# First value tile's depthwise 3x3 convolution: nine VectorE taps and one centring matmul in place of nine diagonal-weight matmuls

## The chip, the cores and the metric

One core of one Trainium2 chip runs the whole program. The metric is the device time of one execution in microseconds (us). The kernel before ran three times: 114.6, 115.24 and 115.32 us, a median of 115.24 us.

## What is computed

The input x has 16 x 16 tokens of 192 channels (12 heads of 16). Two attention blocks run one after the other, each on the group-normalised x and each with x added at the end. Only the first block has the convolution that this document is about. Cut to what matters, for one image:

```python
qkv = gn(x) @ w_qkv.T + b_qkv                      # 256 tokens x 576
q, k, v = split into 12 heads of 16 channels, each a 16 x 16 picture
q = layer_norm(dwconv3x3(q, w_pool_q)) * g_q + b_q # norm over the 16 channels of a head
k = layer_norm(dwconv3x3(k, w_pool_k)) * g_k + b_k
v = layer_norm(dwconv3x3(v, w_pool_v)) * g_v + b_v
attn = softmax(q k^T / 4 + rel_h(q) + rel_w(q))    # 256 x 256 per head
x = x + (attn v + q) @ w_proj.T + b_proj
# the second block has no convolution: LoRA-corrected qkv, the same attention
```

The depthwise convolution multiplies each channel's zero-padded 18 x 18 picture by nine weights at nine shifts and adds the nine products. The layer norm first takes the mean over the 16 channels of a head away ("centring"), which is a multiplication by a fixed 128 x 128 matrix, `centre`.

## The kernel before, in words

Everything lies with channels on partitions and the 256 tokens in the free dimension. The 576 channels of q, k and v are five tiles: A (q, heads 0 to 7), B (k, heads 0 to 7), D (64 rows of q and 64 of k, the last four heads of each), C (v, heads 0 to 7, "the first value tile") and E (v, the last 64 rows). Each engine has its own program, an order written out by hand, and the engines meet at semaphores. Each tile of the first block goes through these steps:

- TensorE projects it (`project`, L739); ScalarE adds the bias and writes it into the padded picture `pad` (`pad_tile`, L446).
- The convolution and the centring. For A and C TensorE does both at once (`convolve`, L750): nine accumulating matmuls whose weights are `centre` with its rows scaled by one tap weight each. VectorE builds these matrices (`tap_matrices`, L612), nine for A and nine for C. For B VectorE does the nine taps itself (`taps`: L635 for the first, L638 for the other eight, each of which adds to the result of the one before and waits for it), and TensorE centres the result with one matmul (`centre_tile`, L781). For D VectorE does five taps and GpSimd four (`convolve_pool`, L311, L316, L319), for E GpSimd does all nine.
- ScalarE squares the centred tile (`tile_stats`, L351), TensorE averages over the head (`variance`, L763), ScalarE takes ln and exp (`tile_rstd`, L356, L358), and VectorE multiplies (`normalise`, L547 and L549) into `full`.
- For q and k, ScalarE and VectorE split `full` in two parts, `hi` (`high`, L452) and `lo` (`low`, L651).

A float32 matmul shows as two records of the trace, so nine matmuls are 18 records.

The attention of a block has three stages of four heads and a last stage. Stage (0, 0) is the first stage of the first block. TensorE's order in it is: `pick_unit` for q (L821, L822; waits for `lo` of A), then what stands under position 0, `rel_unit` 0 and 1 (L840, L843; the relative position terms), `pick_unit` for k, what stands under position 4, four `score` calls (L856). `rel_unit` 0 waits until both ScalarE (L363) and VectorE (`move`, L555) have moved the picked q. ScalarE and VectorE write the position terms beside q (`rel_high`, L368, and `rel_low`, L562). `score` waits for them and for the moved k. VectorE then takes row maxima (`maximum`, L567). `warm_up` (L724) issues matmuls whose results nobody uses.

VectorE's order around the change is: the nine matrices for A; the nine taps of B, each with one matrix of C after it; `normalise(A)`; two casts (L658, L659); `low(A)`, which waits for ScalarE's `high(A)`; taps 0 and 1 of D; then stage (0, 0): `move` q, `normalise(B)`, `low(B)`, `rel_low` twice, `move` k, taps 2 and 3 of D, two maxima, tap 4 of D, two maxima; then `normalise(C)` and stage (0, 1), which begins with `move` q again.

TensorE's convolution of C stands in three pieces: two matmuls before stage (0, 0), three at its position 0 (between `pick_unit` and `rel_unit`), and four at position 4 (between `pick_unit` for k and the scores). After stage (0, 0) come `variance(C)` and `centre_tile(D)`, which waits for the fifth tap of D, then stage (0, 1).

Of the kernel before, what the change touches and what calls it, by code (L numbers as in the profile page):

```python
# [75 lines left out]
def attention_blocks(nc, x_t, w_qkv0, w_qkv1, consts, hots, vectors, neg_hot, rel, lora, v_bias1, w_proj, w_proj_q, out_t):  # L76
    with ExitStack() as ctx:
        def sb(name, shape, dt=F32):
            return ctx.enter_context(nc.sbuf_tensor(name, shape, dt))

        def sem(name):
            return ctx.enter_context(nc.semaphore(name))
# [33 lines left out]
        taps_m = sb("taps_m", [128, 2, TAPS, 128])  # L116
# [4 lines left out]
        conv = sb("conv", [128, 2, TOK])  # L121
# [61 lines left out]
        vtaps_set = sem("vtaps_set")  # L183
# [9 lines left out]
        conv_step = [sem("conv_step_k"), sem("conv_step_d")]  # L193
# [316 lines left out]
        def _(dve):  # L510
# [97 lines left out]
            def tap_matrices(v, first, last):  # L608

                for k in range(first, last):  # L610
                    w = vec[:, TAP0 + 9 * (A, C)[v] + k:TAP0 + 9 * (A, C)[v] + k + 1]
                    dve.tensor_scalar(taps_m[:, v, k, :], centre, w, None,  # L612
                                      ALU.mult).then_inc(vtaps_set if v else qtaps_set, 1)

            tap_matrices(0, 0, TAPS)
# [10 lines left out]
            def taps(t, first, last):  # L626

                s = (B, D).index(t)
# [24 lines left out]
            for k in range(TAPS):  # L653
                taps(B, k, k + 1)
                tap_matrices(1, k, k + 1)
# [4 lines left out]
            low(A)  # L660
            taps(D, 0, 2)
# [57 lines left out]
        def _(pe):  # L719
# [23 lines left out]
            def convolve(t, v, first, last):  # L743

                r = ROWS[t]
                if first == 0:
                    pe.wait_ge(qtaps_set if v == 0 else vtaps_set, TAPS)
                    pe.wait_ge(padded, order0.index(t) + 1)
                for k in range(first, last):
                    mm = pe.matmul(cen_ps[t][0:r, :], taps_m[:, v, k, 0:r],  # L750
                                   pad[:, t, k // 3:k // 3 + SIDE, k % 3:k % 3 + SIDE],
                                   start=(k == 0), stop=(k == TAPS - 1))
                    if k == TAPS - 1:
                        mm.then_inc(centred, 1)
# [10 lines left out]
            def centre_tile(t):  # L765

                r = ROWS[t]
                if t == B:
                    pe.wait_ge(conv_step[0], TAPS)
                    pe.wait_ge(lora_c, 1)  # L770
                    parts = [conv[:, 0, :]]
                elif t == D:
# [258 lines left out]
            convolve(A, 0, 0, TAPS)  # L1031
# [6 lines left out]
            convolve(C, 1, 0, 2)  # L1038
# [10 lines left out]
            stage(0, 0, {0: lambda: convolve(C, 1, 2, 5), 4: lambda: convolve(C, 1, 5, TAPS)})  # L1049
# [110 lines left out]
```

## Time and profile before

| what | value |
|---|---|
| three runs | 114.6, 115.24, 115.32 us |
| median | 115.24 us |
| span of the profiled execution, first to last instruction | 111.6 us |
| median less span | 3.6 us |
| instructions | 2106 |
| TensorE matmul busy in the span | 99.6 us |
| VectorE busy | 64.0 us |
| ScalarE busy | 51.2 us |
| GpSimd busy | 31.0 us |

The profile is one execution. Beside its span no own total is listed for it; the 3.6 us lie between its span and the median of the three runs. A matmul's end in the trace is modelled, so the busy time of TensorE says little of how close it is to its limit; the chain of waits says more. The granted clock is shown as a share of 2.4 GHz: 1.00 is 2.4 GHz and 0.50 is 1.2 GHz.

### The profile page before, as it was taken

Reading aid. Unit: us, or ns where it says so; the run is one execution under the profiler, and the core shown is the slowest. Engines: PE = TensorE matmul, PEld = TensorE weight load, DVE = VectorE, ACT = ScalarE, POOL = GpSimd, SP = SyncE. Lnnn points to the kernel's source line nnn. Section 1 sums busy time; section 2 is a strip of 40 time slices with the busy share of each in tenths; the row PEclk is TensorE's granted clock in tenths of the full one; section 3 lists DMA queues with packets and bytes.
Section 4 is the critical chain, followed back from the end, with each engine's and each line's share of the span. In section 5 each row is a group of like instructions: output and inputs, shape, how many; then the busy total and the mean of one; then the engine's idle time right before and its main releaser. Section 6 shows DMA issues by size and latency. Waiting matters only on the chain.

```text
span 111.6 us, 2106 instructions
## 1 busy us (share of the span) xinstructions
PE 99.6 (89%) x830; PEld 72.2 (65%) x833; DVE 64.0 (57%) x132; ACT 51.2 (46%) x115; POOL 31.0 (28%) x45
## 2 busy tenths in 40 slices
PE   5762999999996999999999999799989999989790
PEld 2211888478885888668657655498659778846550
DVE  0479879767969694944380034455796295580130
ACT  4010181764414793555634642155255648824621
POOL 8269140299999999000000000000000000000000
PEclk9995579999679999999999999999999999999999
DMA  3999930000000000000000000000000000000002
GB/s 74 317 293 301 221 28 0 0 3 6 0 0 0 0 9 0 0 0 6 0 0 0 0 0 6 0 0 0 0 0 6 0 0 6 0 0 0 0 6 71
DMA packets 2826, 3.77 MB, mean 34 GB/s; under 512 B 305, under 2 KB 2225, under 8 KB 2817
## 3 DMA queue, kind: packets, MB, share of 16 engines
q0 software_dynamic: 784, 0.79, 6.3%
q1 hardware_dynamic: 1280, 1.41, 4.6%
q10 hardware_dynamic: 752, 1.44, 4.5%
q8 instruction: 7, 0.11, 0.5%
q14 instruction: 3, 0.02, 0.0%
HBM read 3.44 MB, written 0.20 MB: 33 GB/s over the span
## 4 chain that ended last, share of the span: by engine, by line
PE 78%; DVE 10%; ACT 5%; DMA 3%; issue 2%
PE bank L907 10%; PE bank L750 9%; PE bank L739 9%; PE bank L843 6%; PE bank L840 6%; PE bank L882 5%; PE bank L856 4%; PE bank L895 4%; PE bank L883 4%; DVE xn L541 4%; PE bank L821 4%; DVE mx L567 3%; DMA x<-x_t 3%; PE bank L724 3%; PE bank L822 3%; PE bank L781 2%
## 5 line engine op out<-in xcount | busy, mean ns | idle before, releaser
L567 DVE TENSOR_REDUCE mx<-bank 128x2 fp32r<-128x512 f32 x24 | 15.0, 683 | 5.7 <-PE bank L856 5.7
L378 ACT ACTIVATE pt<-bank 128x512 f32<-128x512 f32 x24 | 13.0, 594 | 7.5 <-PE bank L883 7.3
L882 PE MATMUL bank<-qs,ks 128*128 128x256 f32 x48 | 13.4, 310 | 0.3 <-ACT pt L378 0.2
L739 PE MATMUL bank<-xn,w 96*128 96x256 f32 (+1 forms) x40 | 10.1, 443 | 3.6 <-DVE xn L541 3.6
L562 DVE SCALAR_TENSOR_TENSOR qs<-qs,vec,bank 64x512 fp32r<-64x512 f32 x12 | 8.8, 738 | 6.7 <-ACT qs L368 6.7
L883 PE MATMUL bank<-mt,nhot_r 128*128 128x256 f32 x48 | 11.9, 281 | 0.0
L316 POOL TENSOR_SCALAR tap_p<-pad,vec 64x256 f32<-64x256 f32 (+1 forms) x11 | 10.8, 977 | 0.0
L750 PE MATMUL bank<-pad,taps_m 128*128 128x256 f32 x36 | 10.7, 453 | 0.0
L882 PEld LDWEIGHTS bank<-qs,ks 128*128 128x128 f32 x48 | 9.0, 187 | 2.5 <-ACT pt L378 1.8
L724 PE MATMUL bank<-warm 128*128 128x512 bf16 x28 | 9.0, 443 | 1.5 <-POOL warm L275 1.3
L739 PEld LDWEIGHTS bank<-xn,w 96*128 96x128 f32 (+1 forms) x40 | 6.0, 190 | 6.6 <-issue 4.0
L368 ACT ACTIVATE qs<-bank 64x512 fp32r<-64x512 f32 x12 | 7.1, 591 | 6.0 <-PE bank L843 6.0
L750 PEld LDWEIGHTS bank<-pad,taps_m 128*128 128x128 f32 x36 | 8.3, 233 | 1.5
L883 PEld LDWEIGHTS bank<-mt,nhot_r 128*128 128x128 f32 x48 | 9.0, 188 | 0.1
L574 DVE TENSOR_TENSOR on<-os_,srec 128x256 f32<-128x256 f32 x4 | 1.7, 417 | 12.0 <-ACT srec L389 12.0
L843 PE MATMUL bank<-qs,rel_w 64*32 64x32 f32 x192 | 8.3, 194 | 0.0
L319 POOL TENSOR_TENSOR conv_p<-conv_p,tap_p 64x256 f32<-64x256 f32 (+1 forms) x11 | 8.0, 724 | 0.9
L840 PE MATMUL bank<-qs,rel_w 64*64 64x64 f32 x96 | 7.6, 222 | 0.6 <-issue 0.5
L856 PE MATMUL bank<-ks,qs 128*128 128x256 f32 x48 | 7.7, 299 | 0.0
L840 PEld LDWEIGHTS bank<-qs,rel_w 64*64 64x64 f32 x96 | 6.5, 135 | 1.6 <-ACT ks L363 0.7
L821 PE MATMUL bank<-hi,pick 128*128 128x256 f32 x24 | 7.5, 338 | 0.0
L843 PEld LDWEIGHTS bank<-qs,rel_w 64*32 64x32 f32 x192 | 7.3, 111 | 0.0
(103 smaller groups left out, 170.7 us busy)
## 6 DMA issues: line engine op xcount, KB each, us to landing
ks<-hots POOLq DMA_DIRECT2D x1, 768.0 KB, 9.2
wp<-w_proj ACTq DMA_DIRECT2D x1, 576.0 KB, 8.1
w<-w_qkv SPq DMA_DIRECT2D x1, 432.0 KB, 8.6
w<-w_qkv SPq DMA_DIRECT2D x1, 288.0 KB, 4.8
cst<-consts ACTq DMA_DIRECT2D x1, 256.0 KB, 5.0
nhot<-neg_hot ACTq DMA_DIRECT2D x1, 256.0 KB, 5.8
x<-x_t SPq DMA_DIRECT2D x1, 192.0 KB, 3.2
wpq<-w_proj_q ACTq DMA_DIRECT2D x1, 192.0 KB, 8.9
```

What stands on the lines that cost most here:

```text
L378: act.activation(pt[:, h, :, :], key_banks[h % 2][:, :].rearrange("p (k n) -> p k n", k=QT), ACT.Exp).then_inc(exped[b], 1)
L567: dve.tensor_reduce(mx[:, h, :], ring_bank(h // 4, 4 + h % 4)[:, :].rearrange("p (q n) -> p q n", q=QT), AXX, ALU.max).then_inc(maxed[b], 1)
L724: pe.matmul(to[:, :], warm[:, 0:128], warm[:, :], start=True, stop=True)
L739: mm = pe.matmul((qkv_ps if b == 0 else qkv1_ps)[i][p:p + width, :], w[:, k, col:col + width], xn[:, k, :], start=(k == 0), stop=(k == 1))
L750: mm = pe.matmul(cen_ps[t][0:r, :], taps_m[:, v, k, 0:r], pad[:, t, k // 3:k // 3 + SIDE, k % 3:k % 3 + SIDE], start=(k == 0), stop=(k == ...
L821: pe.matmul(dst, pick[:, v, i:i + 2, :], hi[:, place3[t], :], start=True, stop=False)
L840: pe.matmul(out[:, 64 * i:64 * i + 64], rel_w[64:128, 2 * b, SIDE - 1 - y, 0:64], heads[:, :, y, :], start=True, stop=False, skip_group_ch ...
L843: mm = pe.matmul(by_x[:, x], rel_w[64:128, 2 * b + 1, SIDE - 1 - x, 0:32], heads[:, x, 8 * r:8 * r + 8, :], start=False, stop=True, skip_g ...
L856: mm = pe.matmul(ring_bank(g, n)[:, q * TOK:(q + 1) * TOK], qs[:, h, q * 128:(q + 1) * 128], ks[:, h, :], start=True, stop=True)
L882: pe.matmul(dst, ks[:, h, k * 128:(k + 1) * 128], qs[:, h, :], start=True, stop=False)
L883: mm = pe.matmul(dst, nhot_r[:, j, :], mt[:, g, :], start=False, stop=True)
L907: mm = pe.matmul(y_ps[t], weights, moving, start=first_y[b][t], stop=stop, skip_group_check=True)
```

## The change

VectorE builds no matrices for C. It does nine taps for C itself, six after the taps of B and ahead of `normalise(A)`, three after `low(A)` and ahead of the taps 0 and 1 of D. The result goes to a third slot of `conv`. TensorE's nine matmuls for C go: the two ahead of stage (0, 0) leave nothing, the three at position 0 leave one `warm_up` matmul, the four at position 4 leave one centring matmul that waits for the nine taps. The taps of B follow each other with nothing between them. A's convolution stays with TensorE.

```diff
--- before.py
+++ after.py
@@ -113,12 +113,12 @@
         b_row = lo_w[:, 2 * DIM + 32:].rearrange("p (b n) -> p b n", b=2)
         wp = sb("wp", [128, 2, HG, DIM])
         wpq = sb("wpq", [128, 2, DIM])
-        taps_m = sb("taps_m", [128, 2, TAPS, 128])
+        taps_m = sb("taps_m", [128, TAPS, 128])
         pick = sb("pick", [128, 4, 8, 64], F32R)
         warm = sb("warm", [128, 512], mybir.dt.bfloat16)
 
         pad = sb("pad", [128, 5, PADDED, PADDED])
-        conv = sb("conv", [128, 2, TOK])
+        conv = sb("conv", [128, 3, TOK])
         conv_p = sb("conv_p", [128, 2, TOK])
         tap_p = sb("tap_p", [128, 2, TOK])
         cen_e = sb("cen_e", [64, TOK])
@@ -180,7 +180,6 @@
         ones_set = sem("ones_set")
         picks_set = sem("picks_set")
         qtaps_set = sem("qtaps_set")
-        vtaps_set = sem("vtaps_set")
         rel_hi = sem("rel_hi")
         rel_split = sem("rel_split")
         rel_set = sem("rel_set")
@@ -190,7 +189,7 @@
         lora_w = sem("lora_w")
         w1_set = sem("w1_set")
         padded = sem("padded")
-        conv_step = [sem("conv_step_k"), sem("conv_step_d")]
+        conv_step = [sem("conv_step_k"), sem("conv_step_d"), sem("conv_step_v")]
         p_tap = sem("p_tap")
         p_sum = sem("p_sum")
         e_copied = sem("e_copied")
@@ -605,14 +604,9 @@
             dve.wait_ge(d_cst, 16)
             dve.wait_ge(d_vec, 16)
 
-            def tap_matrices(v, first, last):
-
-                for k in range(first, last):
-                    w = vec[:, TAP0 + 9 * (A, C)[v] + k:TAP0 + 9 * (A, C)[v] + k + 1]
-                    dve.tensor_scalar(taps_m[:, v, k, :], centre, w, None,
-                                      ALU.mult).then_inc(vtaps_set if v else qtaps_set, 1)
-
-            tap_matrices(0, 0, TAPS)
+            for k in range(TAPS):
+                w = vec[:, TAP0 + 9 * A + k:TAP0 + 9 * A + k + 1]
+                dve.tensor_scalar(taps_m[:, k, :], centre, w, None, ALU.mult).then_inc(qtaps_set, 1)
 
             dve.wait_ge(d_rel, 16)
             dve.tensor_copy(relt_hi[64:128], relt[64:128]).then_inc(rel_hi, 1)
@@ -625,7 +619,7 @@
 
             def taps(t, first, last):
 
-                s = (B, D).index(t)
+                s = (B, D, C).index(t)
                 dst = conv[:, s, :].rearrange("p (a c) -> p a c", a=SIDE)
                 for k in range(first, last):
                     src = pad[:, t, k // 3:k // 3 + SIDE, k % 3:k % 3 + SIDE]
@@ -650,14 +644,14 @@
                 dve.wait_ge(hi_set[0], i + 1)
                 dve.tensor_tensor(lo[:, i, :], full[:, t, :], hi[:, i, :].bitcast(F32), ALU.subtract).then_inc(lo_set[0], 1)
 
-            for k in range(TAPS):
-                taps(B, k, k + 1)
-                tap_matrices(1, k, k + 1)
+            taps(B, 0, TAPS)
+            taps(C, 0, 6)
             normalise(A)
             dve.wait_ge(d_nhot, 16)
             dve.tensor_copy(ident_r[:], ident).then_inc(id_set, 1)
             dve.tensor_copy(nhot_r[:], nhot[:].rearrange("p (j n) -> p j n", j=4)).then_inc(id_set, 1)
             low(A)
+            taps(C, 6, TAPS)
             taps(D, 0, 2)
 
             def k_in():
@@ -740,18 +734,14 @@
                                        start=(k == 0), stop=(k == 1))
                 mm.then_inc(projected[b], 1)
 
-            def convolve(t, v, first, last):
-
-                r = ROWS[t]
-                if first == 0:
-                    pe.wait_ge(qtaps_set if v == 0 else vtaps_set, TAPS)
-                    pe.wait_ge(padded, order0.index(t) + 1)
-                for k in range(first, last):
-                    mm = pe.matmul(cen_ps[t][0:r, :], taps_m[:, v, k, 0:r],
-                                   pad[:, t, k // 3:k // 3 + SIDE, k % 3:k % 3 + SIDE],
+            def convolve(t):
+
+                pe.wait_ge(qtaps_set, TAPS)
+                pe.wait_ge(padded, order0.index(t) + 1)
+                for k in range(TAPS):
+                    mm = pe.matmul(cen_ps[t], taps_m[:, k, :], pad[:, t, k // 3:k // 3 + SIDE, k % 3:k % 3 + SIDE],
                                    start=(k == 0), stop=(k == TAPS - 1))
-                    if k == TAPS - 1:
-                        mm.then_inc(centred, 1)
+                mm.then_inc(centred, 1)
 
             def variance(t):
                 r = ROWS[t]
@@ -769,6 +759,9 @@
                     pe.wait_ge(conv_step[0], TAPS)
                     pe.wait_ge(lora_c, 1)
                     parts = [conv[:, 0, :]]
+                elif t == C:
+                    pe.wait_ge(conv_step[2], TAPS)
+                    parts = [conv[:, 2, :]]
                 elif t == D:
                     pe.wait_ge(conv_step[1], D_SPLIT)
                     pe.wait_ge(p_sum, TAPS - D_SPLIT)
@@ -1028,14 +1021,13 @@
             pe.wait_ge(d_w0, 32)
             project(0, 0, A, w0)
             project(0, 1, B, w0)
-            convolve(A, 0, 0, TAPS)
+            convolve(A)
             project(0, 2, C, w0)
             variance(A)
             project(0, 3, D, w0)
             centre_tile(B)
             project(0, 4, E, w0)
             variance(B)
-            convolve(C, 1, 0, 2)
 
             def q_and_e():
                 pe.wait_ge(w1_set, 2)
@@ -1046,7 +1038,7 @@
                 variance(E)
                 add_input(0, 0)
 
-            stage(0, 0, {0: lambda: convolve(C, 1, 2, 5), 4: lambda: convolve(C, 1, 5, TAPS)})
+            stage(0, 0, {0: lambda: warm_up(1, bank[7]), 4: lambda: centre_tile(C)})
             variance(C)
             centre_tile(D)
             warm_up(1, bank[5])
```

## Rows read from the trace of the kernel before

**Rows 1.** The page: TensorE clock granted, 40 slices of 2.79 us, in tenths

```profile
PEclk9995579999679999999999999999999999999999
```

**Rows 2.** The page: the chain that ended last, by engine and line

```profile
PE 78%; DVE 10%; ACT 5%; DMA 3%; issue 2%
PE bank L907 10%; PE bank L750 9%; PE bank L739 9%; PE bank L843 6%; PE bank L840 6%; PE bank L882 5%; PE bank L856 4%; PE bank L895 4%; PE bank L883 4%; DVE xn L541 4%; PE bank L821 4%; DVE mx L567 3%; DMA x<-x_t 3%; PE bank L724 3%; PE bank L822 3%; PE bank L781 2%
```

**Rows 3.** That chain in order of time, 18 to 40 us: start us, us, what

```profile
23.23 0.86 PE bank L750 x4
...
24.68 1.30 PE bank L750 x6
...
26.06 0.62 PE bank L840 x8
...
29.02 3.40 PE bank L750 x8
...
32.70 1.29 DVE mx L567 x2
33.98 0.61 DVE conv L638
...
37.76 0.58 PE bank L840 x8
```

**Rows 4.** VectorE in order of time: start us, us, what, [idle before]

```profile
14.75 0.48 DVE L635 TENSOR_SCALAR conv<-pad,vec 128x256 f32<-128x256 f32 x1 [1.19 <-ACT pad L446]
...
19.29 0.28 DVE L612 TENSOR_SCALAR taps_m<-cst,vec 128x128 f32<-128x128 f32 x1
19.48 0.48 DVE L638 SCALAR_TENSOR_TENSOR conv<-pad,vec,conv 128x256 f32<-128x256 f32 x1
...
20.94 0.42 DVE L547 TENSOR_TENSOR nrm<-bank,rstd 128x256 f32<-128x256 f32 x1 [0.78 <-ACT rstd L358]
21.40 0.41 DVE L549 TENSOR_SCALAR full<-nrm,vec 128x256 f32<-128x256 f32 x1
...
23.45 0.42 DVE L651 TENSOR_TENSOR lo<-full,hi 128x256 fp32r<-128x256 f32 x1 [0.96 <-ACT hi L452]
23.79 0.82 DVE L635 TENSOR_SCALAR conv<-pad,vec 128x256 f32<-128x256 f32 x1
24.65 0.58 DVE L638 SCALAR_TENSOR_TENSOR conv<-pad,vec,conv 128x256 f32<-128x256 f32 x1
25.27 0.69 DVE L555 CAST qs<-bank 64x512 fp32r<-64x512 f32 x1
...
30.39 1.24 DVE L638 SCALAR_TENSOR_TENSOR conv<-pad,vec,conv 128x256 f32<-128x256 f32 x2
32.70 1.29 DVE L567 TENSOR_REDUCE mx<-bank 128x2 fp32r<-128x512 f32 x2 [1.07 <-PE bank L856]
```

**Rows 5.** ScalarE in order of time, the same columns

```profile
19.55 0.48 ACT L446 ACTIVATE pad<-bank,vec 128x256 f32<-128x256 f32 x1 [0.48 <-PE bank L739]
...
28.27 0.59 ACT L368 ACTIVATE qs<-bank 64x512 fp32r<-64x512 f32 x1 [0.42 <-PE bank L843]
```

**Rows 6.** GpSimd in order of time, the same columns

```profile
21.69 1.04 POOL L311 TENSOR_SCALAR conv_p<-pad,vec 128x256 f32<-128x256 f32 x1 [6.62 <-ACT pad L446]
22.72 0.92 POOL L316 TENSOR_SCALAR tap_p<-pad,vec 128x256 f32<-128x256 f32 x1
```

**Rows 7.** TensorE in order of time, the same columns

```profile
10.44 3.75 PE L739 MATMUL bank<-xn,w 96*128 96x256 f32 x8 [2.99 <-DVE xn L541]
...
20.90 0.70 PE L781 MATMUL bank<-conv,cst 128*128 128x256 f32 x2
```

**Rows 8.** Stretches: busy of each engine, granted clock, DMA share, GB/s

```profile
8.50:9.00 0.50, 0.00 (x0) 0.00 (x0) 0.50 (x1) 0.00 (x0) 0.50 (x1) 0.50 0.93 289
26.00:28.30 2.30, 2.21 (x49) 2.13 (x49) 1.78 (x4) 0.97 (x3) 2.05 (x4) 1.00 0.04 7
29.00:32.30 3.30, 3.30 (x10) 2.58 (x9) 2.53 (x4) 0.59 (x1) 3.13 (x5) 0.50 0.00 0
```

## The prediction, made before the changed kernel ran

> **What bounds the kernel now.** I read four views in this order. First the page's chain by engine and line: TensorE is 78% of it, and L750, the convolution matmuls for A and C, is 9% of the span [rows 2]. That makes the change look like a gain, so the next question is what stands beside those matmuls. The chain in order of time shows C's three pieces: 0.86 us at 23.23 (4 records), 1.30 us at 24.68 (6 records) and 3.40 us at 29.02 (8 records) [rows 3]. Third, VectorE in order of time over the same stretch: from 14.75 to the first row maximum at 32.70 it is nearly full. Three idle times matter there: 0.78 us ahead of `normalise(A)`, 0.96 ahead of `low(A)`, and 1.07 ahead of the maxima, the only one that C's matmuls cause [rows 4]. And `rel_unit` 0 at 26.06 starts just after VectorE has moved q (25.27 + 0.69 = 25.96) [rows 3, 4]: the 1.30 us piece only fills a wait for VectorE. Last, the granted clock: it is low in slices 10 and 11 [rows 1], and in 29.00 to 32.30 it is 0.50 against 1.00 during the position terms before it [rows 8]. So the 3.40 us piece runs at 1.2 GHz, 0.425 us a record against 0.217 in the 1.30 us piece. After the maxima the chain goes through tap 4 of D (VectorE) back to TensorE [rows 3].
>
> So in 20 to 37 us VectorE and TensorE bound the kernel in turn, and the change takes work from TensorE and gives it to VectorE there.
>
> **The change, part by part.** All times are those of the profiled execution.
>
> *Taps of B without the matrices.* Between two taps stands a matrix today; the pitch is 0.59 us (19.29 and 19.48 are the last such pair, the tap before them starts 0.59 before 19.48) [rows 4]. Without it each tap waits for the one before. No row has two free dependent taps in succession, but `normalise` shows a dependent pair: 20.94 + 0.42 = 21.36, and the next starts at 21.40, a gap of 0.04 [rows 4]. I take 0.48 + 0.04 = 0.52. Bounds: 0.59 (the matrix costs nothing) and 0.40 (the issue interval of a tap ahead of a matrix). B then ends at 14.75 + 8 x 0.52 + 0.48 = 19.39 instead of 19.96. Nobody gains: `centre_tile(B)` starts at 20.90 in TensorE's own order [rows 7].
>
> *Six taps of C ahead of `normalise(A)`.* They need C's picture, which ScalarE writes from 19.55 for 0.48 [rows 5]: start about 20.07. Of the 0.57 us won on B nothing is left. GpSimd starts its own taps at 21.69 [rows 6], and VectorE's taps are slower from then: two in 1.24, 0.62 each [rows 4]. Three at 0.52 and three at 0.62 end at about 23.47. `normalise(A)` starts there instead of at 20.94: 2.5 late. Bounds for the nine C taps: 0.40 each (no gap, no slowdown) and 0.82 each, the longest tap of the trace (23.79) [rows 4].
>
> *`normalise(A)` to `low(A)`.* The two multiplications take 0.87 us to 24.34, the two casts 0.7 more to about 25.05 (now from 21.81 to 23.45 - 0.96 = 22.49 [rows 4]). ScalarE's `hi` of A (about 0.48, as the ScalarE row of that tile size [rows 5]) is then done under the casts, so the 0.96 wait goes. `low(A)` starts at 25.05 instead of 23.45: 1.6 late. TensorE's `pick_unit` waits for that.
>
> *Three taps of C, then taps 0 and 1 of D, ahead of `move` q.* 3 x 0.62 = 1.86 from 25.45 gives 27.3; the D taps take 1.44 as now (23.79 to 25.23), to 28.75. `move` q starts at 28.77 instead of 25.27 and `rel_unit` 0 at 29.55 instead of 26.06: **3.5 late**. This is the step that counts. TensorE can't hide it: behind the waiting `rel_unit` are the pick of k and the scores, all of which need it or come after it in its order. ScalarE's `rel_high` and GpSimd (whose results for D and E nobody awaits here) don't set it.
>
> *Nine matmuls out of TensorE.* The first piece (0.86) lay ahead of a pick that now waits for `low(A)`: worth nothing. The second (1.30) lay in the wait for `move` q: nothing, and its warm-up of one matmul is hidden. The third, 3.40, gives way to one centring matmul (two records, 0.70 at the most [rows 7], twice that at the low clock). Without it the scores could have started once k had been moved, just ahead of 30.39, and VectorE's next two D taps ran until 31.63 (30.39 + 1.24) [rows 4]. So what the third piece costs today is the idle 1.07 us up to 32.70, and that is what is won. The other 2.3 us of it lay beside VectorE's work.
>
> *Sum with the clock high.* 3.5 - 1.07 = +2.4 us at the maxima. Nothing later absorbs it: two maxima, tap 4 of D, two maxima, `normalise(C)` and `move` q run back to back on VectorE and `rel_unit` at 37.76 awaits them [rows 3]; after it the chain is TensorE nearly throughout [rows 2].
>
> *The clock.* In the changed kernel TensorE idles from the end of `variance(B)` (23.23, where C's first piece stands now) to 29.55, but for one pick (0.6, now 24.09 to 24.68) and a warm-up [rows 3]. The trace has one idle time of that kind: 2.99 us ahead of 10.44 [rows 7], and within it, at 8.50, the clock is at 0.50 [rows 8]; it is still low in slice 4 [rows 1]. It fell also after 2.3 us of position terms [rows 8]. So I take it that the two `rel_unit` run at 1.2 GHz. No row has them there. They take 2.2 us now (26.06 to ScalarE's start behind them at 28.27 [rows 3, 5]). Bounds: nothing more, and 2.1 more (0.425 against 0.217 a record, times 1.96, as for C's own matmuls [rows 3]). I take **+1.9**, near the upper end, because the only matmuls seen at both clocks scale so, and a little less because some of the 2.2 us is latency. It is on the path: ScalarE's second `rel_high` at 28.27 was released by them (L843 [rows 5]), and `rel_low` and `move` k follow. The scores at half clock lie beside VectorE's D taps and maxima.
>
> *Sum:* 3.5 - 1.07 + 1.9 = +4.3. The profiled span 111.6 becomes 115.9. The median of the runs lies 3.6 above the span, so 115.24 + 4.3 = **119.5 us**.
>
> *A rule weighed.* The GpSimd rows and the taps beside them show taps of 0.62 instead of 0.48 [rows 4, 6], some 0.1 us for each. The Trainium skill ("SBUF — State Buffer", section "SBUF: two separate sides") says of the port pair that VectorE and GpSimd share that one of them holds it for its whole instruction, and that it holds also for a VectorE instruction with two SBUF inputs against a GpSimd one that reads SBUF. That speaks against the change; what it would make here is the third rival.
>
> **The rivals.**
>
> 1. *The clock stays high.* For it: the clock is not shown falling at once in an idle time, and the picks and the warm-up matmul stand in this one. Against: 8.50. Time: 115.24 + 2.4 = 117.6.
>
> 2. *TensorE is the bound after all, and the change is faster.* The place is the start of `rel_unit` 0. It decides if VectorE moves q less than 1.07 us late; then the loss is smaller than the idle time that goes. For it: 78% TensorE in the chain [rows 2]. At the extreme all 5.56 us of L750 for C go and 0.9 of centring and warm-up come: 110.6. Against: with C's taps at 0.40 each, `normalise(A)` starts at 22.5, `low(A)` at 24.1, and with 0.4 each for the five taps after it `move` q at 26.5, 1.2 late. Even the low bound is 115.24 + 0.15 = 115.4 with the clock high. To be faster, taps would have to be cheaper than any row shows.
>
> 3. *Each contended tap waits out a GpSimd instruction.* Six taps of C run beside GpSimd instructions of some 0.9 us [rows 6]; met half-way through they would wait 0.45 instead of the 0.1 counted, 6 x 0.35 = 2.1 more: 121.6. For it: the tap of 0.82 at 23.79. (This is the rule of the Trainium skill's page "SBUF — State Buffer" named above; the trace agrees with it in that tap only.) Against: 0.58 and twice 0.62 in the same traffic [rows 4].
>
> 4. *The low clock lasts.* If the picks, the scores and the next pair of position terms also run at 1.2 GHz, and the latter (2.1 us now, from 37.76) take the same +1.9, the time is 121.4. Against: the clock rose both times after some us of dense matmuls (slices 5 and 12 [rows 1]), and centring, scores and variance are such.
>
> **How the numbers follow.** 0.50 for the forecast (119.5; its own range 118.4 to 120.5), 0.25 for the first rival (117.6), 0.05 for the second with its low bound, 0.08 for the third, 0.12 for the fourth. The range 116.8 to 121.5 takes in the high clock with slightly cheaper taps and reaches the two dear cases. A measurement of this kernel can tell about 1%, 1.15 us, from no change. Slower by more than that: 0.92; within 1%: 0.05, the low bound of the second rival; faster: 0.03.
>
> **What would show it.** In the changed profile: the first C tap at about 20.1 released by ScalarE's `pad`; free taps 0.52 apart and contended ones 0.62; `normalise(A)` at 23.5; no wait ahead of `low(A)`; `move` q near 28.8 and `rel_unit` 0 near 29.6; two idle times of TensorE, of 2 and 3 us, both ended by VectorE (L651, L555); a clock of 0.50 at 29.6 and `rel_unit` pairs of about 4 us; the maxima at about 37 instead of 32.7 with no idle time ahead of them; everything after 37.76 later by one constant. It is wrong if `rel_unit` 0 starts before 27.5, if the shift at the maxima is under 1 us, or if a wait after 40 us swallows it.

## The result, and the profile after

The changed kernel has a median of 121.62 us in four runs (120.32 to 122.14) against 115.28 us of the kernel before in the same rounds: ratio 1.058, interval 1.047 to 1.069. The forecast was 119.5 us with a range of 116.8 to 121.5. The direction was right and the time lies just above the range. A second set of rounds (below, `after_again`) gave 1.067, interval 1.058 to 1.075. The change costs some 6%, where I had forecast 3.7%. A ratio here compares the runs of each kernel that lie within 1.5% of its own fastest, in the same rounds.

The page of the changed kernel first. What was L739 is L733, L750 is L742, L781 is L774, L840 and L843 are L833 and L836, L856 is L849, L895 is L888, L907 is L900, L635 is L629, L638 is L632.

```profile
span 118.9 us, 2074 instructions
...
PE   5795999931989999999999999899989999999790
...
PEclk9999999985555899999999999999997559999999
...
PE 72%; DVE 13%; ACT 6%; issue 4%; DMA 3%
PE bank L900 10%; PE bank L733 6%; PE bank L849 6%; PE bank L833 6%; PE bank L836 6%; PE bank L875 5%; PE bank L888 4%; PE bank L876 4%; PE bank L742 4%; DVE xn L540 3%; PE bank L814 3%; DMA x<-x_t 3%; PE bank L718 3%; PE bank L815 2%; DVE conv L632 2%
```

In the chain L742, now A's convolution alone, has 4% where L750 had 9% [rows 2]: the work did leave the chain. "issue" went from 2% to 4% and VectorE from 10% to 13%. In the TensorE row slices 8 and 9 (counted from 0) show 3 and 1 tenths: the waits. And the clock row has two low spells, slices 8 to 13 and 30 to 32, where the kernel before had slices 3 to 5 and 10 to 11 [rows 1].

The first spell is what the prediction had priced. The chain in order of time (start, us, what):

```profile
20.40 0.36 DVE conv L629
...
27.50 1.97 issue
29.47 1.03 PE bank L833 x8
30.50 0.83 PE bank L836 x16
31.33 0.88 PE bank L833 x8
32.21 0.84 PE bank L836 x16
...
41.96 0.58 PE bank L833 x8
```

VectorE's taps are in the chain now (20.40). `rel_unit` 0 starts at 29.47 behind 1.97 us of "issue" that stand for the wait for VectorE's move of q; the two `rel_unit` take 1.03 + 0.83 + 0.88 + 0.84 = 3.58 us instead of 2.2 [rows 3]. Stage (0, 1) starts at 41.96 instead of 37.76 [rows 3]: 4.2 us late, where 4.3 was forecast.

VectorE in the same stretch (start, us, what, idle before):

```profile
15.44 4.13 DVE L632 SCALAR_TENSOR_TENSOR conv<-pad,vec,conv 128x256 f32<-128x256 f32 x8
20.40 0.35 DVE L629 TENSOR_SCALAR conv<-pad,vec 128x256 f32<-128x256 f32 x1 [0.83 <-ACT pad L445]
...
23.37 0.42 DVE L546 TENSOR_TENSOR nrm<-bank,rstd 128x256 f32<-128x256 f32 x1
...
24.44 0.94 DVE L652 CAST nhot_r<-nhot 128x512 fp32r<-128x512 f32 x1
25.31 0.41 DVE L645 TENSOR_TENSOR lo<-full,hi 128x256 fp32r<-128x256 f32 x1
25.64 2.00 DVE L632 SCALAR_TENSOR_TENSOR conv<-pad,vec,conv 128x256 f32<-128x256 f32 x3
...
28.67 0.69 DVE L554 CAST qs<-bank 64x512 fp32r<-64x512 f32 x1
...
36.39 1.29 DVE L566 TENSOR_REDUCE mx<-bank 128x2 fp32r<-128x512 f32 x2
```

Eight dependent taps of B take 4.13 us, 0.516 each (forecast 0.52). `normalise(A)` starts at 23.37 (forecast 23.5), `low(A)` at 25.31 with no idle time ahead of it (25.05), `move` q at 28.67 (28.77), the maxima at 36.39 with no idle time ahead of them (about 37) [rows 4 for the kernel before].

From there to 87 us the two kernels run alike: `rel_unit` 0 of stages (0, 2), (1, 0) and (1, 1) stands at 52.27, 79.68 and 87.61 in the timeline of TensorE, against 48.06, 75.46 and 83.37 before, each 4.2 us late. Then the other 3.1 us come, in one place. The chain of the changed kernel around 91 us (start, us, what):

```profile
90.80 0.12 PE bank L876
90.92 1.95 PE bank L900 x4
...
94.88 1.71 PE bank L849 x8
96.58 1.52 PE bank L888 x16
```

The same chain of the kernel before, at the same place of the program:

```profile
86.65 1.03 PE bank L907 x4
...
88.83 0.94 PE bank L856 x8
89.78 1.00 PE bank L895 x16
```

The four passes of L900 (L907 before) take 1.95 us for 1.03, the scores of L849 1.71 for 0.94, L888 1.52 for 1.00, and the stretch between them is slower likewise. The granted clock says why. Two rows around the two `rel_unit` of stage (0, 0) and one from here (busy time of each engine, clock, DMA share, GB/s):

```profile
26.00:29.00 3.00, 0.86 (x4) 0.71 (x4) 2.86 (x6) 0.59 (x1) 2.83 (x4) 0.50 0.01 3
29.50:33.00 3.50, 3.50 (x49) 3.46 (x49) 2.10 (x4) 1.01 (x2) 3.37 (x4) 0.50 0.02 5
...
90.80:97.60 6.80, 6.80 (x34) 4.68 (x36) 2.64 (x5) 1.97 (x4) 0.00 (x0) 0.50 0.00 0
```

TensorE is busy all of the 6.80 us from 90.80 and has a clock of 0.50. At the same place of the kernel before it is at 1.00 [rows 1]. Stage (1, 2) then starts at 99.74 instead of 92.42: 7.3 us late, which is the difference of the two spans (118.9 and 111.6). Nothing of the change stands near 91 us.

So there are two questions: is the first 4.2 us what the prediction says it is, and does the second spell belong to the change?

### The profile page after: what moved, and what is told of

The parts are those of the page before. It is cut to its first block, busy times and chain, and to the rows that moved or that the text cites. A ratio compares the mean times of both kernels' runs of the same rounds, so it can differ in the third digit from the quotient of the medians.

```text
span 118.9 us, 2074 instructions
## 1 busy us (share of the span) xinstructions
PE 104.3 (88%) x814; PEld 74.6 (63%) x818; DVE 67.0 (56%) x132; ACT 51.4 (43%) x115; POOL 31.7 (27%) x45
## 2 busy tenths in 40 slices
DMA packets 2824, 3.75 MB, mean 32 GB/s; under 512 B 304, under 2 KB 2224, under 8 KB 2816
## 3 DMA queue, kind: packets, MB, share of 16 engines
q10 hardware_dynamic: 752, 1.44, 4.3%
## 4 chain that ended last, share of the span: by engine, by line
PE 72%; DVE 13%; ACT 6%; issue 4%; DMA 3%
PE bank L900 10%; PE bank L733 6%; PE bank L849 6%; PE bank L833 6%; PE bank L836 6%; PE bank L875 5%; PE bank L888 4%; PE bank L876 4%; PE bank L742 4%; DVE xn L540 3%; PE bank L814 3%; DMA x<-x_t 3%; PE bank L718 3%; PE bank L815 2%; DVE conv L632 2%
## 5 line engine op out<-in xcount | busy, mean ns | idle before, releaser
L377 ACT ACTIVATE pt<-bank 128x512 f32<-128x512 f32 x24 | 13.1, 594 | 9.1 <-PE bank L876 9.0
L875 PE MATMUL bank<-qs,ks 128*128 128x256 f32 x48 | 14.1, 323 | 0.3 <-ACT pt L377 0.2
L876 PE MATMUL bank<-mt,nhot_r 128*128 128x256 f32 x48 | 12.6, 292 | 0.0
L733 PE MATMUL bank<-xn,w 96*128 96x256 f32 (+1 forms) x40 | 10.1, 443 | 2.0 <-DVE xn L540 2.0
L718 PE MATMUL bank<-warm 128*128 128x512 bf16 x28 | 9.9, 478 | 1.5 <-POOL warm L274 1.3
L833 PE MATMUL bank<-qs,rel_w 64*64 64x64 f32 x96 | 8.5, 234 | 3.1 <-issue 3.1
L632 DVE SCALAR_TENSOR_TENSOR conv<-pad,vec,conv 128x256 f32<-128x256 f32 x20 | 10.4, 521 | 0.6
L833 PEld LDWEIGHTS bank<-qs,rel_w 64*64 64x64 f32 x96 | 7.3, 149 | 3.8 <-issue 2.6
L849 PE MATMUL bank<-ks,qs 128*128 128x256 f32 x48 | 9.1, 339 | 0.3 <-DVE ks L554 0.3
L733 PEld LDWEIGHTS bank<-xn,w 96*128 96x128 f32 (+1 forms) x40 | 6.0, 189 | 5.3 <-issue 2.8
L836 PE MATMUL bank<-qs,rel_w 64*32 64x32 f32 x192 | 9.0, 198 | 0.0
L849 PEld LDWEIGHTS bank<-ks,qs 128*128 128x128 f32 x48 | 7.9, 235 | 1.8 <-DVE qs L561 1.4
L836 PEld LDWEIGHTS bank<-qs,rel_w 64*32 64x32 f32 x192 | 8.0, 118 | 0.0
```

The costliest lines, as they stand in the source:

```text
L377: act.activation(pt[:, h, :, :], key_banks[h % 2][:, :].rearrange("p (k n) -> p k n", k=QT), ACT.Exp).then_inc(exped[b], 1)
L632: dve.scalar_tensor_tensor(out=dst, in0=src, scalar=w, in1=dst, op0=ALU.mult, op1=ALU.add).then_inc(conv_step[s], 1)
L718: pe.matmul(to[:, :], warm[:, 0:128], warm[:, :], start=True, stop=True)
L733: mm = pe.matmul((qkv_ps if b == 0 else qkv1_ps)[i][p:p + width, :], w[:, k, col:col + width], xn[:, k, :], start=(k == 0), stop=(k == 1))
L833: pe.matmul(out[:, 64 * i:64 * i + 64], rel_w[64:128, 2 * b, SIDE - 1 - y, 0:64], heads[:, :, y, :], start=True, stop=False, skip_group_ch ...
L836: mm = pe.matmul(by_x[:, x], rel_w[64:128, 2 * b + 1, SIDE - 1 - x, 0:32], heads[:, x, 8 * r:8 * r + 8, :], start=False, stop=True, skip_g ...
```

## The experiments

The executions of one program differ. The kernel before has a span near 111.5 us (110.9 to 112.8) most often, but also others from 113 to 121 us. In the profiles the place, the number and the length of the low spells differ: the one of 6.8 us at 91 us costs 3.1 us, two of 13 and 10 us in another profile of the changed kernel (`after_again`) cost some 10. So a profile shows one execution, and the ratios tell about the kernel. Ratios are to the kernel before in the same rounds.

**1. The waits filled.** Warm-up matmuls in TensorE's two waits of the first block, and nothing else:

```diff
             variance(B)
+            warm_up(8, bank[7])
...
-            stage(0, 0, {0: lambda: warm_up(1, bank[7]), 4: lambda: centre_tile(C)})
+            stage(0, 0, {0: lambda: warm_up(10, bank[7]), 4: lambda: centre_tile(C)})
```

> The changed kernel with 8 warm-up matmuls ahead of the first pick of q and 10 instead of 1 behind it, both inside TensorE's two waits for VectorE (2.2 and 2.6 us). If the clock is what makes the two rel_unit slow (prediction: +1.9 us of the shift), the clock stays at 1.00 up to 33 us, the two rel_unit take 2.2 us instead of 3.6, and rel_unit of stage (0, 1) starts some 1.5 to 1.9 us earlier than in the changed kernel (near 40.2 instead of 41.96). If VectorE alone sets the shift, it starts at 42 as before. For the whole time: 121.6 - 1.7 = 119.9 if the low spell of the second block is independent of this, 116.8 to 118 if that spell goes too.

> The changed kernel with TensorE's two waits filled by 17 more warm-up matmuls, again. The shift at stage (0, 1) was 2.4 us in its profile, as the prediction's sum with the clock high. If the first block's long low spell is what makes the rest, its fastest runs are at 114.1 to 115.5 and its median 1 to 2 us under the changed kernel's; if the second block's spell comes as often as in the changed kernel, no run is below 117.

The first four runs have spans of 115.5 to 120.3 us and a median of 120.33 us; in the profile the two `rel_unit` take 2.22 us and stage (0, 1) starts at 40.24, both as expected. The second set has a median of 117.54 us and a ratio of 1.028 (1.022 to 1.034); all six spans lie between 113.7 and 115.4, where the ten runs of the changed kernel lie between 118.0 and 125.6. The chain in the profile of `filled_again` (start, us, what):

```profile
25.62 2.17 PE bank L718 x10
...
28.59 0.62 PE bank L833 x8
29.21 0.55 PE bank L836 x16
29.76 0.47 PE bank L833 x8
30.23 0.58 PE bank L836 x16
...
40.09 0.58 PE bank L833 x8
```

Its stretches (busy time of each engine, clock, DMA share, GB/s):

```profile
26.00:31.00 5.00, 4.21 (x59) 2.99 (x58) 4.33 (x8) 1.32 (x4) 4.66 (x6) 1.00 0.02 5
31.50:38.00 6.50, 5.67 (x17) 3.85 (x17) 6.33 (x11) 1.86 (x4) 6.17 (x8) 0.50 0.00 0
86.00:98.00 12.00, 12.00 (x158) 10.13 (x156) 7.19 (x13) 7.32 (x15) 0.00 (x0) 1.00 0.01 3
```

The ten warm-up matmuls at 25.62 end before `rel_unit` 0 can start, so they cost nothing. The clock is 1.00 until 31 us, the two `rel_unit` take 0.62 + 0.55 + 0.47 + 0.58 = 2.22 us, and stage (0, 1) starts at 40.09, 2.3 us after the kernel before (37.76 [rows 3]); the prediction's sum with the clock high was 2.4. That the two agree so well is luck, because the 2.3 hides a difference ahead of the change: C's padding starts between 18.8 and 20.5 us in the profiles here. Measured from it, the maxima start 2.0 us later than before (15.2 for 13.1 us) and stage (0, 1), by its start in TensorE's timeline, 2.9 us later (21.0 for 18.1), where the changed kernel is 3.3 and 3.9 us later (16.5 and 22.0). The clock falls all the same at some 31 us, behind the position terms, and the 0.9 us between the maxima and stage (0, 1) go to that. From 86 to 98 us it is 1.00. So 17 matmuls whose results nobody uses, put into the first block, take away half of the loss and more in the second set. Ahead of stage (0, 1) that is 1 us, which the profiles show. The part behind is gone, or nearly, in seven of ten runs by their spans; that it is gone because the waits were filled isn't shown, since an addition far behind this place does something like it (experiment 5).

**2. TensorE's nine matmuls kept.** VectorE's taps stay, TensorE does its old work too (with A's matrices, its result overwritten by the centring):

```diff
             variance(B)
+            keep(0, 2)
...
-            stage(0, 0, {0: lambda: warm_up(1, bank[7]), 4: lambda: centre_tile(C)})
+            stage(0, 0, {0: lambda: keep(2, 5), 4: lambda: (keep(5, TAPS), centre_tile(C))})
```

> The changed kernel with TensorE's nine matmuls kept at their three old places beside the new centring matmul; they use A's matrices and their result is overwritten, so it is VectorE's nine taps alone that are new on the path. If TensorE's work bounded this stretch, it costs 3 us over the changed kernel at the maxima. By the prediction's account it costs nothing there, or gains: the kept matmuls lie in TensorE's waits, shorten the low clock, and stage (0, 1) starts at 40 to 42 (changed kernel 41.9).

> The changed kernel with TensorE's nine matmuls kept beside VectorE's taps, again. If more TensorE work is really the faster of the two, its fastest group lies near 114 and its median 2 us or more under that of after_again in the same rounds; if the first comparison was luck of the runs, both medians agree within 1 us.

The ratios are 1.022 (1.014 to 1.030) and 1.030 (1.021 to 1.038): with all of its old TensorE work the changed kernel is 3 to 4% faster than without it (1.058 and 1.067). Seven of twelve spans are 113.7 to 114.8. So VectorE's taps with the matmuls kept cost 2 to 3%, and taking the matmuls away costs 3 to 4% more. Both profiles fell on runs in which the clock was low in the third piece. That of `after_keep_pe`:

```profile
27.15 1.30 PE bank L750 x6
28.45 1.67 issue
30.12 0.62 PE bank L840 x8
...
34.36 3.37 PE bank L750 x8
37.73 0.43 PE bank L781 x2
...
38.44 1.29 DVE mx L566 x2
```

The second piece (27.15, 1.30 us) leaves only 1.67 us of wait ahead of `rel_unit` 0, and the first of the two runs its first half at the high clock (0.62). The third piece takes 3.37 us and delays the maxima to 38.44, against 36.39 in the changed kernel. C's padding starts 0.6 us later here (20.53 for 19.89), so 1.4 us of that are the kept work's, which is the idle time of VectorE ahead of these maxima (1.42, released by the scores). So in such a run the kept work does cost at the maxima, against my account, and stage (0, 1) starts at 43.25, outside the expected 40 to 42. The runs at 114 us have no profile, so where their clock was low isn't known: one of the seven has a mean granted clock of 1.000, two have 0.985 and four 0.952 to 0.955, and the profile of `after_pool_waits` (below) has 0.955 with a low spell from 26 to 37 us.

**3. C's taps late.** All nine just ahead of the maxima:

```diff
-            taps(C, 0, 6)
...
-            taps(C, 6, TAPS)
...
-            stage(0, 0, {0: k_in, 2: lambda: taps(D, 2, 4), 3: lambda: taps(D, 4, D_SPLIT)})
+            stage(0, 0, {0: k_in, 2: lambda: (taps(D, 2, 4), taps(C, 0, TAPS)), 3: lambda: taps(D, 4, D_SPLIT)})
```

> The changed kernel with all nine taps of C moved behind taps 2 and 3 of D in stage (0, 0), just ahead of the maxima, and the centring of C behind the third score. If what counts is the late move of q (prediction's step of 3.5 us), rel_unit 0 is back at 26 us, the clock stays high through it, and stage (0, 1) starts clearly earlier than 41.96. If VectorE's total work up to the maxima is what counts, nine taps of 0.6 us less the 1.07 us idle and the low clock's 1.9 us leave stage (0, 1) at 41.5 to 42.3, the same as the changed kernel, with the slip moved from rel_unit 0 to the maxima.

Ratio 1.045 (1.037 to 1.054). VectorE in order of time:

```profile
21.29 0.42 DVE L546 TENSOR_TENSOR nrm<-bank,rstd 128x256 f32<-128x256 f32 x1 [2.05 <-ACT rstd L357]
...
23.80 0.43 DVE L645 TENSOR_TENSOR lo<-full,hi 128x256 fp32r<-128x256 f32 x1 [0.97 <-ACT hi L451]
...
25.62 0.69 DVE L554 CAST qs<-bank 64x512 fp32r<-64x512 f32 x1
...
34.03 5.51 DVE L632 SCALAR_TENSOR_TENSOR conv<-pad,vec,conv 128x256 f32<-128x256 f32 x8
39.58 1.29 DVE L566 TENSOR_REDUCE mx<-bank 128x2 fp32r<-128x512 f32 x2
```

Neither half of the expectation holds as it stands. `move` q is back at 25.62, but `rel_unit` runs at the low clock here too (26.41 to 30.0), the maxima start at 39.58, 3.2 us later than in the changed kernel, and stage (0, 1) at 45.80 instead of 41.5 to 42.3. The wait for `rstd` of A is 2.05 us (0.78 in the kernel before, where the matrices stretched the taps of B [rows 4]) and that for `hi` of A 0.97: the changed kernel had put six taps into the first, and the second was gone. VectorE's total isn't the whole account; which of its waits the taps fill counts as well. That the whole kernel is still no slower than the changed one (1.045 against 1.058, in other rounds, with intervals that overlap) suggests that most of what separates them is decided behind this stretch. The profile is of a run with a span of 122.8 us; three of the five runs lie at 117.3 to 118.0.

**4. GpSimd held back.** Its convolutions start after C's taps:

```diff
             pool.wait_ge(padded, n_padded[D])
+            pool.wait_ge(conv_step[2], TAPS)
```

> The changed kernel with GpSimd's convolutions of D and E started only after the nine taps of C. If GpSimd slows VectorE's taps by 0.10 us each, as the prediction counted, six of them get 0.6 us shorter in all and rel_unit 0 starts some 0.7 us earlier (near 28.7 instead of 29.47); by the full-instruction hold of the port it would be 2 us or more. The rest of the shift stays.

```profile
24.14 0.42 DVE L653 CAST nhot_r<-nhot 128x512 fp32r<-128x512 f32 x1
...
24.91 1.52 DVE L633 SCALAR_TENSOR_TENSOR conv<-pad,vec,conv 128x256 f32<-128x256 f32 x3
...
27.42 0.69 DVE L555 CAST qs<-bank 64x512 fp32r<-64x512 f32 x1
```

From the padding of C to `rel_unit` 0 there are 28.21 - 19.83 = 8.38 us, in the changed kernel 29.47 - 19.89 = 9.58: 1.2 us less. Three taps of C take 1.52 us instead of 2.00 (0.16 each), the six ahead of `normalise(A)` only 0.1 less in all (2.87 for 2.97 to its start), so the nine taps gain 0.6, what the prediction had counted for them. The other half is not in the taps: the cast of `nhot` (L653, L652 in the changed kernel) takes 0.42 instead of 0.94, the largest single piece, and the second multiplication of `normalise(A)` 0.41 instead of 0.57.

The full-instruction hold of the Trainium skill ("SBUF — State Buffer", "SBUF: two separate sides") had given 2 us and more by the expectation; the trace doesn't agree, with 1.2 in all and 0.6 for the taps. The profiled run has no low spell in the second block and a span of 114.0; the other three have 117.6 to 117.9. With both this and the kept matmuls (`keep_pe_pool_waits`):

> VectorE's nine taps with TensorE's nine matmuls kept beside them, and GpSimd's convolutions started after C's taps. By the run with GpSimd late, 1.2 us of the wait for move q goes; by the run with the matmuls kept, the low clock of the first block is short or absent. Both together: stage (0, 1) some 20 us behind the padding of C (changed kernel 22.0, before 18.1), spans of 112.8 to 113.5 in runs without a low spell in the second block. If the two don't add, 114.

Stage (0, 1) starts at 38.53, 19.1 us behind the padding of C (before: 18.1, changed kernel: 22.0, GpSimd held back alone: 20.3), better than the 20 expected. In this profile the clock is at 1.00 through the whole of stage (0, 0), which it isn't in the profiles of either edit alone, so how much each gives here can't be told apart. The clock is low from 86 to 93 us instead. The spans are 113.2, 115.5, 115.7 and 119.1.

**5. The second block moved.** More warm-up matmuls between the blocks, in the changed kernel and in the kernel before:

```diff
-            warm_up(5, bank[2])
+            warm_up(13, bank[2])
             group_sums(1)
```

> The changed kernel with 8 more warm-up matmuls of 0.22 us between the two blocks, 1.7 us of added TensorE work on the critical path. Theory 1: the second block's low spell (90.8 to 97.6 us, 3.1 us of loss) comes from where the position terms of stage (1, 1) lie in time against the instants at which the clock is set; a shift of 1.7 us moves them away: no low spell, 121.6 + 1.7 - 3.1 = 120.2. Theory 2: the changed kernel's second block has the spell wherever it lies: 121.6 + 1.7 = 123.3.

> The kernel before with 20 more warm-up matmuls between the two blocks, some 4.3 us, which brings its second block to the same time as in the changed kernel with nothing else changed. Theory 1 (place in time): the low spell appears near 91 us, 115.3 + 4.3 + 3.1 = 122.7. Theory 2 (the spell is a consequence of what the change does in the first block): none, 119.6.

> The changed kernel with 4 more warm-up matmuls between the blocks (0.86 us; half of the 8 that took the second block's low spell away in three of four runs). Theory 1 (where the second block lies in time decides): the spell is in some runs and not in others, spans in two groups some 3 us apart, near 116 and 119.5. Theory 3 (any added dense work between the blocks holds the clock): no spell, span 116.

> The same with 16 more warm-up matmuls (3.45 us). Theory 1: the second block lies anew; as far as the kernel before (half of its runs have a spell) and the one shifted by 20 (three of four) tell, most runs have it: spans near 118.6 without and 121.8 with it. Theory 3 (dense work between the blocks holds the clock, the more the better): none has it, all near 118.6.

> The changed kernel with 8 more warm-up matmuls between the blocks, again. Ten runs of the changed kernel had spans of 118.0 to 125.6 us, none near 115; three of four of this one had 116.8 with 1.7 us more work. If where the second block lies decides (theory 1), most runs are again at 116.8 and the median stays below that of the changed kernel. If those three were luck, most are at 119.7 or more (118.0 + 1.7).

| warm-up matmuls added | added us | spans |
|---|---|---|
| changed kernel, none | 0 | 118.0 to 125.6, ten runs |
| 4 | 0.86 | 123.3 to 123.9, four |
| 8 | 1.7 | 116.7, 116.8, 117.0, 126.0 |
| 8, again | 1.7 | 117.4, 117.9, 118.2, 122.2, 122.3, 123.8 |
| 16 | 3.45 | 121.8, 121.8, 123.0, 128.9 |
| kernel before, 20 | 4.3 | 115.0, 119.1, 119.2, 121.8 |

Time doesn't rise with the work added: 4 matmuls give 5 to 6% more than 8 (ratios 1.103 and 1.040, the latter 1.050 the second time), and 16 give 1.093 (1.076 to 1.110). Theory 3 (dense work between the blocks holds the clock) is out. The profile with 4 added has a spell from 54 to 65 us, ahead of the added work (76 us), beside the one at 96 us:

```profile
54.50:64.00 9.50, 9.50 (x53) 7.08 (x51) 2.11 (x5) 4.40 (x9) 0.00 (x0) 0.50 0.00 0
```

The programs with 4 and with 8 added are the same up to there, and the first profile with 8 has no spell at 54 us, while the second has one. So theory 1, that where the second block lies decides, isn't shown: part of what separates these sets is decided ahead of the moved work, by what differs from run to run, and the sets ran in different rounds. The repetition has 122 us and more in three of six. The kernel before, moved by 20, has some 4 us more than its best in two of four and 7 in one.

Its profile shows such a difference in the first block. Up to 67 us its program is the kernel before, yet the clock stays at 1.00 there, C's third piece takes 0.22 us a record instead of 0.425 (its last six records below), and VectorE has no idle time ahead of the maxima, where the profile before has 1.07 us [rows 4]:

```profile
29.66 1.46 PE L750 MATMUL bank<-pad,taps_m 128*128 128x256 f32 x6
...
32.04 1.29 DVE L567 TENSOR_REDUCE mx<-bank 128x2 fp32r<-128x512 f32 x2
```

**6. Dense work inside the second block.** Two warm-up matmuls between the `rel_unit` of stage (1, 1); in the kernel before also one matmul of C moved between those of stage (0, 0).

> The changed kernel with two more warm-up matmuls (0.43 us) between the two rel_unit of stage (1, 1), and nothing else. Theory 1 (the second block's low spell is made by the thin stretch of position terms just ahead of it, wherever the instants fall): no low spell at 91 us, span 118.9 + 0.4 - 3.1 = 116.2. Theory 2 (it is a consequence of the first block or of the run): the spell stays, span 119.3.

> The kernel before with one of C's matmuls moved between the two rel_unit of stage (0, 0), and two warm-up matmuls between those of stage (1, 1). If dense work between the position terms holds the clock, the low spell at 29 us is gone, C's third piece takes 1.3 us instead of 3.40, stage (0, 1) starts at 36.8 to 37.3 instead of 37.76, and the span is 111.6 - 0.7 + 0.4 = 111.3, with fewer of its runs at 114 and 117. If one matmul isn't enough, the spell stays and the span is 112.2.

Neither held the clock. `after_dense` has a ratio of 1.061 (1.053 to 1.069), like the changed kernel, and its profile is low from 89 to 96 us and again from 102 to 107. `before_dense` is at 0.999 (0.990 to 1.009), and its clock still falls at 29 us. GpSimd held until D's second tap in the kernel before made no difference that can be told, 1.003 (0.991 to 1.015):

> The kernel before with GpSimd's convolutions held until tap 1 of D is done on VectorE (near 25.2 us). The contention ahead of move q goes (0.82 and 0.58 us taps to 0.5 each), some 0.4 us earlier for move q; C's second piece of matmuls ends at 25.97 and takes over as what rel_unit waits for. Expected: 0 to 0.2 us faster than before, within what can be measured. If GpSimd's results for E come too late for stage (0, 2), slower by up to 1 us.

No version tried beats the kernel before.

**7. The changed kernel again.**

> The changed kernel unchanged, on the same chip and in the same rounds as the next one. Theory 1 (the shift is 3.6 us without a low spell in the second block and some 7 with one, and which it is depends on how the instants at which the clock is set fall in that run): spans in groups, 115 and 118 to 119, not one value; most in the upper group. Theory 2 (the change always costs 7 us): all at 118 to 120. Profile: stage (0, 1) at 41 to 42 in either case.

Ratio 1.067 (1.058 to 1.075), spans 118.5, 118.7, 119.7, 120.2, 125.3 and 125.6. Theory 1 wanted some runs near 115; there are none in ten. Stage (0, 1) starts at 41.41 in its profile, so the first 4 us are nearly the same (3.7), and all of its profile's further loss lies behind, in low spells at 54 to 67 and 95 to 105 us. So neither theory holds as it was put.

## Why the prediction was right or wrong

- *Taps of B without matrices, 0.52 each, nobody gains:* right (0.516; `centre_tile(B)` at its old place in TensorE's order).
- *`move` q and `rel_unit` 0 later by 3.5 us:* nearly right, 3.4 (29.47 for 26.06), of which 0.3 is C's padding, later by that much ahead of the change.
- *GpSimd's slowdown:* right for C's taps, 0.6 in all, though by luck in its parts: 0.16 each for the last three and next to nothing for the first six, where I took 0.10 for six of the nine. Holding GpSimd back gave 1.2, because the cast of `nhot` and the multiplication ahead of it lose 0.7; I took the cast from the row of the kernel before, where it lost only 0.2 (0.62 for 0.42). It didn't show in the time because taps 0 and 1 of D took 1.1 us (27.56 to 28.67) instead of the 1.44 counted.
- *The third piece of matmuls is worth 1.07 us:* right for this profile. In the filled kernel `rel_unit` 0 is 3.1 us late and the maxima 2.0, both from C's padding. But these matmuls have that price only where they meet a low clock: in the profile of `before_shift20`, with the same program up to there and the clock high, the idle time isn't there. In such a run their removal wins nothing.
- *The two `rel_unit` at 1.2 GHz, +1.9:* the mechanism is right and shown by filling the waits; the size is 1.4 (3.58 for 2.16). With it the sum at the maxima is 3.4 - 1.07 + 1.4 = 3.7, and 3.7 were measured (36.39 for 32.70), not 4.3. Another 0.5 us come between the maxima and stage (0, 1), where the scores, the variance and the centring of D run at the low clock (35.37 to 39.6) and VectorE waits for the pick of q; the prediction had these lie beside VectorE's work and cost nothing. So the 4.2 at stage (0, 1), or 3.9 from C's padding, agrees with the 4.3 partly by luck: one term was 0.5 too large and one of 0.5 was left out.
- *The rival of TensorE as the bound* is out: removing its work made the kernel slower, and putting it back made it faster by 3 to 4%.
- *"Nothing later absorbs it", "everything after 37.76 later by one constant":* this step failed. Nothing is absorbed, but 3 us are added, at 91 us in the first profile. The fourth rival had the low clock last from the first block into stage (0, 1) and gave 121.4 for it; the time is nearly that, by luck, because the place isn't: the clock was back at 1.00 at 39.6 and fell again 51 us later. I had priced the clock only where the change makes a wait. I had also read the spread of the kernel before from three runs (114.6 to 115.32); with more runs it has a group at 114 to 115 of span and single ones at 120, so further low spells were to be expected there as well.
- *The third rival, by which each contended tap waits out a GpSimd instruction:* out, by the 0.6 us of experiment 4. Its support, the tap of 0.82 (L635), reads one tile only, the padded picture; the taps that read two tiles (L638) took 0.58 and 0.62 there [rows 4].

What brings the further spell about is settled only this far. It isn't in VectorE's taps as such: with the waits filled (seven of ten runs) or the matmuls kept (at least seven of twelve), most runs are without it by their spans, where the changed kernel has it in ten of ten. That makes the waits of the first block a likely part of it, but 8 matmuls between the blocks, far behind the waits, take it away in at least three of ten runs too, and two in the second block don't. How a wait at 24 to 29 us makes a low spell at 54 or 91 us likelier, when the clock was at 1.00 for 15 to 50 us between, isn't shown by any run. Nor is it the change's alone: the kernel before with GpSimd held back has one from 49 to 59 us in its profile. What is shown is the step that failed and its size: 3.1 us behind 42 us in the first profile, where the prediction had nothing. Its cause stays open.

## What to carry to other kernels

Dense matmuls that fill TensorE's waits can be worth keeping even when their results could be had elsewhere: here their removal cost more (3 to 4%) than the nine VectorE taps that replaced them (2 to 3%), and 17 idle warm-up matmuls won half of the loss back. Before moving work off an engine whose granted clock can fall, ask what it did while it waited, ask whether an idle time that the change would win was itself made by a low clock, and price the clock for the whole program, not for the stretch of the change. And where the runs of a kernel differ by low spells, compare many runs: a profile is one of them.

## What the runs showed of the hardware that was not expected

The clock fell in stretches where TensorE's row is full. Ahead of the fall at 91 us stand 2.2 us of small matmuls of position terms, as ahead of that at 29 us in the kernel before, and dense matmuls between them didn't change that: two in `after_dense`, where the clock falls at 89 us, and one in `before_dense`, where it falls at 29. But the same 2.2 us stand in every stage of position terms, mostly without a fall: at 83.37 us of the kernel before the clock stays at 1.00, and the same program falls at 29 us in one profile and not in that of `before_shift20`.

The granted clock isn't always recorded at the start. The eight projections of A and B take the same 3.75 us in both kernels, 0.47 us a record, where the same form takes 0.22 at a clock of 1.00 (C's projection in the changed kernel: 4 records in 0.88 us of the chain at 18.99), but the clock column (the third number from the end) has 0.50 for the kernel before and 1.00 for the changed one. The stretch in the changed kernel:

```profile
10.50:14.00 3.50, 3.37 (x8) 2.65 (x9) 3.17 (x12) 0.48 (x1) 0.90 (x3) 1.00 1.84 241
```

the same stretch of the kernel before:

```profile
10.50:14.00 3.50, 3.50 (x9) 2.67 (x10) 2.99 (x12) 0.48 (x1) 0.90 (x3) 0.50 1.91 239
```

and TensorE of the changed kernel in order of time, the same line as in [rows 7]:

```profile
10.63 3.75 PE L733 MATMUL bank<-xn,w 96*128 96x256 f32 x8 [1.43 <-DVE xn L540]
```

So slices 3 and 4 and a part of 5 of the changed kernel's clock row say 9 where the clock was low; durations of a known form are the better witness. The mean clock of a run is off by the same amount, which is one reason why a higher mean clock doesn't always go with a shorter span.

Of the instructions compared in experiment 4, a plain cast of 512 float32 columns loses most beside GpSimd: 0.42 us without it, 0.62 (kernel before) and 0.94 (changed kernel) with it. Three dependent taps of 256 columns take 1.52 us without it and 2.00 with it.
